# Moving the next group's first scores and their softmax inside the attention bodies of a six-stage graph network

## The chip, the cores and the metric

One core of a Trainium2 chip runs the whole program as one launch. The metric is the device time of one execution in microseconds. The engines are TensorE (PE in the rows; PEld are its weight loads), VectorE (DVE), ScalarE (ACT), GpSimd (POOL) and SyncE (SP, which issues all DMAs here). Each works through an instruction list of its own and waits on semaphores that the others raise.

## What is computed

128 graphs of 64 nodes with 384 features pass through four residual blocks. Each block normalises x, takes its positive part h, computes a graph layer on it and adds the result to x:

```
h = relu(layernorm(x));  x = x + L0(h, adj)      # two graph-convolution layers
h = relu(layernorm(x));  x = x + L1(h, adj)      # attention, 12 heads of 32, edges masked by adj
h = relu(layernorm(x));  x = x + L2(h, adj)      # two directed graph-convolution layers
h = relu(layernorm(x));  x = x + L3(h, adj)      # attention, 12 heads, adj as a bias, output projection
```

The change lies in L1 and L3. In both, q, k and v are projections of h, the scores of each graph and head are softmaxed over 64 keys and multiplied with v. L3 projects the outcome once more (Wo, bo); L1 does not.

## The kernel before, in words

**Stages and groups.** There are six stages (two gnn, att1, two gcn, att3), each a sweep over 16 groups of eight graphs. A group has T = 4 tiles of 128 rows, two graphs each. In a sweep the body for group g also prepares group F = g + 1 (its projections and first scores) and group X = g + 2 (its normalised, transposed input). A loop turn holds two bodies; 14 bodies run in the loop, and two behind it, of which the first (g = 14) still has an F. In att1 it also has an X, the first group of the stage that follows, and the last group runs in a body of its own that joins the stages (to_gcn); in att3, the last stage, the body for g = 14 has no X and that for g = 15 has neither.

**What sets the order.** The order of each engine's list is written by hand: the function a_body exists once for each engine and calls the steps in the order in which that engine runs them. An engine never goes past an instruction that waits. The waits are stated in the steps: after(engine, name, group, k) waits until step `name` of that group has been done for the k-th time.

**The steps of an attention body.** In TensorE's a_body (L890):

- part(j) (L766, through project, L664) is the j-th of ten projections of F, nine matmuls each: j = 0 to 5 give k and q, j = 6 to 9 give the values of tiles 0 to 3. They go to two PSUM banks by turns, so each waits until what stood in its bank has been read. In att3 part(7) waits for a_add_x(g,1), and part(8) in both stages for a_nat(F,1).
- a_score(g, t) (L813): 48 small matmuls, the scores of tile t, into four PSUM banks of their own. It needs q and k of the group, and that the scores of the tile before have been read.
- a_turn_p(g, t, half) (L834): three transpositions of tile t's softmax weights, which ScalarE copies out (a_keep_p, L1200).
- a_mix(g, t) (L844): the weights times the values.
- a_out(g, t, F, X) (L865): att3's output projection, nine matmuls at L885; in att1 it returns at once. Tile 1 waits for a_keep_o(g,1) and, where there is an X, for low(0).
- a_turn(F, X, c) (L756; turn_next in the body): four transpositions of X's normalised input. For c = 1 it waits in att3 for a_nat(F,0) and for c = 2 for the half of low(1) that VectorE writes.

In VectorE's a_body (L1585):

- a_nat(F, t) (nat in the body, L1491): four copies of tile t's values from PSUM with the bias added (L1502). It waits for part(6 + t).
- split_h (low in the body, L1368): the low half of X's input, one instruction at L1373 in the attention stages.
- a_soft(g, t) (L1523): three scalar_tensor_tensors (L1533) that scale the scores and add the bias, then the maximum over the keys (L1539), and in att3 a maximum of absolute values as well (L1541). GpSimd subtracts the maximum (a_shift, L526), and ScalarE takes the exponential (a_exps, L1198).
- a_sums(g, t) (L1544): in att3 the sum of the exponentials, its reciprocal and a product (L1549 to L1553), by which GpSimd then scales the weights (a_weigh, L534). In att1 it does nothing.
- a_add_x(g, t) (L1575): in att3 the output projection added to x (L1583). In att1 it does nothing.
- a_keep_o(g, t) (L1556): takes the mixed values out of PSUM; in att3 the low half for the output projection (L1561), behind ScalarE's copy (L1210).

The lists of the others in the stretch that matters: GpSimd has a_shift(g,3), a_add(g,1), a_weigh(g,3), a_shift(F,0), a_add(g,2), a_weigh(F,0); ScalarE has the copy of turn_next(1), a_keep_o(g,2), the copy of turn_next(2), a_keep_p(g,3,0), a_exps(F,0), a_keep_p(g,3,1).

The wait that binds part(7) in att3, and the one of part(8):

```
elif j == 7:
    if G.lead:
        emptied(pe, X, 0)
    else:
        after(pe, "xr", G + -1, 1)
else:
    after(pe, "evac_n", G, j - 7)
```

Here "xr" is a_add_x, "evac_n" is a_nat, and G + -1 is the group before F, so g.

Of the kernel before, what the change touches and what calls it, by code (L numbers as in the profile page):

```python
# [146 lines left out]
def graph_layers(nc, x_in, adj, adj_q, adj_t, w_all, v_all, v_cols, beta, masks, x_mid, z_mid, out):  # L147
# [5 lines left out]
    with ExitStack() as ctx:  # L153
# [487 lines left out]
        def _(pe):  # L641
# [171 lines left out]
            def a_score(g, t):  # L813
                if t == 0:
                    after(pe, "evac_t", g, 2 * C - 1)
                if t == 0 and g.lead and not g.third:
                    pe.wait_ge(st["mu"].sem, st["mu"].base[g.n])
                    pe.wait_ge(st["z1"].sem, st["z1"].base[g.n])
                elif t == 0 and g.lead:
                    pe.wait_ge(st["ex"].sem, st["ex"].base[g.n])  # L820
                    pe.wait_ge(st["dT"].sem, st["dT"].base[g.n])
                    pe.wait_ge(st["cc"].sem, st["cc"].base[g.n])
                after(pe, "stt", g, t - 1)
                for c in range(C):
                    for a in (0, 1):
                        own = slice(t * P + a * S, t * P + (a + 1) * S)
                        for j in range(HC):
                            r = slice(j * HD, (j + 1) * HD)
                            mm = nc.tensor.matmul(psum[a * S:(a + 1) * S, 2 + j, c * S:(c + 1) * S],  # L829
                                                  q_T[r, g.par, c, own], k_T[r, g.par, c, own],  # L830
                                                  start=True, stop=True, skip_group_check=True)
                done(mm, "s")

            def a_turn_p(g, t, half):  # L834
                if half == 0:
                    after(pe, "n0" if g.third else "ex", g, t)
                after(pe, "pt", g, 2 * t + half - 1)
                for i in range(3):
                    u = 2 * (3 * half + i)
                    mm = nc.tensor.transpose(tp[:, i * P:(i + 1) * P],  # L840
                                             s_sb[:, t % 2, u:u + 2].rearrange("p h k -> p (h k)"), ident)
                done(mm, "tp")
# [22 lines left out]
            def a_out(g, t, F, X):  # L865


                if not g.third:
                    return
                b = t % 2  # L870
                after(pe, "olo", g, t)
                if not F:
                    after(pe, *(("evac_n", g, T - 1), ("xr", g + -1, T - 1), ("xr", g, 0), ("xr", g, 2))[t])
                elif X:
                    after(pe, *(("evac_t", F, 2), ("lo", X, 0), ("lo", X, 2), ("xr", g, 2))[t])
                else:
                    after(pe, *(("evac_t", F, 2), ("evac_t", F, 4), ("evac_n", F, 0), ("xr", g, 2))[t])
                if t == 0:
                    pe.wait_ge(w_split, 2 * w_total(g.n))
                dst = bank_of(g + 1, Y_SLOT[t])  # L880
                s_ = w_slot(g, 3)
                k = 0
                for c in range(C):
                    for wpart, opart in ((w_hi, o_hi), (w_hi, o_lo), (w_lo, o_hi)):
                        mm = nc.tensor.matmul(dst[:, 0:H], opart[:, b, c * P:(c + 1) * P],  # L885
                                              wpart[s_][:, c, :], start=(k == 0), stop=(k == 3 * C - 1))
                        k += 1
                done(mm, "y")

            def a_body(g, F, X):  # L890
                def part(j):
                    if F:
                        a_part(F, j, X)

                def turn_next(c):
                    if X:
                        a_turn(F, X, c)

                a_turn_p(g, 0, 0)
                part(0)  # L900
                a_turn_p(g, 0, 1)
                a_score(g, 2)
                part(1)
                a_mix(g, 0)
                part(2)
                a_turn_p(g, 1, 0)
                part(3)
                a_turn_p(g, 1, 1)
                a_score(g, 3)
                a_out(g, 0, F, X)  # L910
                part(4)
                a_mix(g, 1)
                part(5)
                a_turn_p(g, 2, 0)
                turn_next(0)
                part(6)
                a_turn_p(g, 2, 1)
                a_out(g, 1, F, X)
                turn_next(1)
                if F:  # L920
                    a_score(F, 0)
                part(7)
                a_mix(g, 2)
                turn_next(2)
                a_turn_p(g, 3, 0)
                part(8)
                a_turn_p(g, 3, 1)
                if F:
                    a_score(F, 1)
                a_out(g, 2, F, X)  # L930
                if g.third:
                    a_mix(g, 3)
                    part(9)
                else:
                    part(9)
                    a_mix(g, 3)
                a_out(g, 3, F, X)
# [395 lines left out]
        def _(dve):  # L1333
# [189 lines left out]
            def a_soft(g, t):  # L1523

                b = t % 2
                third = g.third
                if t == 0 and third:
                    dve.wait_ge(ld["adj_in"].sem(g), ld["adj_in"].at(g))
                bias = adjc if third else biasc
                after(dve, "s", g, t)  # L1530
                after(dve, "tp", g, 2 * t - 3)
                for c in range(C):
                    ins = nc.vector.scalar_tensor_tensor(  # L1533
                        out=s_sb[:, b, c * HC:(c + 1) * HC], in0=s_bank[:, :, c * S:(c + 1) * S],
                        scalar=SCALE3 if third else SCALE1,
                        in1=bias[:, g.par, t].unsqueeze(1).to_broadcast([P, HC, S]), op0=ALU.mult, op1=ALU.add)
                done(ins, "stt")
                after(dve, "stt", g, t)
                done(nc.vector.tensor_reduce(mx[:, b], s_sb[:, b], AX.X, ALU.max), "mxr")  # L1539
                if third:  # L1540
                    done(nc.vector.tensor_reduce(am[:, b], s_sb[:, b], AX.X, ALU.max,  # L1541
                                                 apply_absolute_value=True), "absr")

            def a_sums(g, t):  # L1544

                b = t % 2
                if g.third:
                    after(dve, "ex", g, t)
                    done(nc.vector.tensor_reduce(sums[:, b], s_sb[:, b], AX.X, ALU.add), "sm")  # L1549
                    after(dve, "sm", g, t)  # L1550
                    done(nc.vector.reciprocal(sums[:, b], sums[:, b]), "rc")
                    after(dve, "rc", g, t)
                    done(nc.vector.scalar_tensor_tensor(out=rinv[:, b], in0=am[:, b], scalar=0.0,  # L1553
                                                        in1=sums[:, b], op0=ALU.is_gt, op1=ALU.mult), "ri")
# [30 lines left out]
            def a_body(g, F, X):  # L1585
                def low(c):
                    if X:
                        split_h(F, X, c)

                def nat(t):  # L1590
                    if F:
                        a_nat(F, t)
                if X:
                    stats_of(X, 0)
                a_sums(g, 1)
                if X:
                    stats_of(X, 1)
                a_soft(g, 2)
                if X:
                    shift_of(X)  # L1600
                a_keep_o(g, 0)
                next_w(F, X, 0)
                a_sums(g, 2)
                a_soft(g, 3)
                a_add_x(g, 0)
                if F:
                    a_bias(F)
                a_keep_o(g, 1)
                next_w(F, X, 1)
                low(0)  # L1610
                nat(0)
                a_sums(g, 3)
                a_add_x(g, 1)
                low(1)
                if F:
                    a_soft(F, 0)
                nat(1)
                a_keep_o(g, 2)
                low(2)
                if F:  # L1620
                    a_sums(F, 0)
                nat(2)
                if F:
                    a_soft(F, 1)
                a_add_x(g, 2)
                a_keep_o(g, 3)
                nat(3)
                a_add_x(g, 3)
# [273 lines left out]
```

## Time and profile before

| what | value |
|---|---|
| median of 3 runs | 3032.25 us (3029.55 to 3032.59) |
| the profiled execution | 3030.7 us, of which the span from first to last instruction is 3028.6 us |
| TensorE busy | 2803.1 us (93%) |
| VectorE busy | 1964.6 us (65%) |
| ScalarE busy | 1032.5 us (34%) |
| GpSimd busy | 950.6 us (31%) |

A row of a timeline gives the start in us, the duration in us, the engine, the source line, the operation, what it writes and reads, the shapes and how many instructions were merged; in brackets stands how long the engine had been idle before it and what ended that. Matmuls are pipelined, so a row may begin a little before the one above it has ended. "issue" is a wait that the profile does not explain. A granted clock of 1.00 is 2.4 GHz, 0.50 is 1.2 GHz.

### The profile page before, as it was taken

How to read it: one execution, taken by the hardware profiler on the slowest of the kernel's cores; microseconds unless marked ns; L12 is line 12 of the kernel's file. 1: busy time of each engine (PE TensorE's matmuls, PEld its weight loads, DVE VectorE, ACT ScalarE, POOL GpSimd, SP SyncE). 2: the span in 40 equal slices, each digit the busy share in tenths (PEclk: the TensorE clock that was granted, in tenths of full speed). 3: DMA queues.
4: the chain of work that ended last, by engine and by line, in shares of the span. 5: the costliest groups of instructions: out<-in, count | busy, mean ns of one | idle time of the engine just before them, and what ended most of it. 6: DMA issues, size and time to landing. Idle time of an engine off the chain costs nothing.

```text
span 3028.6 us, 71986 instructions
## 1 busy us (share of the span) xinstructions
PE 2803.1 (93%) x26048; PEld 2341.8 (77%) x26048; DVE 1964.6 (65%) x4550; ACT 1032.5 (34%) x1985; POOL 950.6 (31%) x874
## 2 busy tenths in 40 slices
PE   6999999999989999999999998999998899999997
PEld 5888878888877777777877777778776677777776
DVE  3444445555576666677676666677767777777775
ACT  2444433333334444443332322222222333433342
POOL 1121214444433333332010110334333343443443
PEclk9999999999999999999999999999999899999999
DMA  3222332333311211122211223222332011111111
GB/s 92 76 74 77 98 91 91 104 104 104 112 54 47 66 51 47 47 84 64 68 57 56 68 74 107 67 82 83 99 99 82 29 42 47 47 47 41 36 30 34
DMA packets 197214, 210.20 MB, mean 69 GB/s; under 512 B 72736, under 2 KB 197024, under 8 KB 197024
## 3 DMA queue, kind: packets, MB, share of 16 engines
q1 hardware_dynamic: 197024, 207.33, 22.2%
q8 instruction: 161, 2.64, 0.4%
q14 instruction: 29, 0.24, 0.0%
HBM read 131.80 MB, written 75.50 MB: 68 GB/s over the span
## 4 chain that ended last, share of the span: by engine, by line
PE 70%; DVE 15%; issue 10%; POOL 2%; ACT 2%; DVEq 1%; DMA 0%; SPq 0%; POOLq 0%; ACTq 0%
PE psum L672 26%; PE psum L675 25%; PE psum L723 3%; DVE v_x L1502 3%; PE psum L990 3%; PE psum L660 2%; PE psum L840 2%; DVE room L1650 2%; PE psum L829 2%; PE psum L885 2%; DVE room L1533 2%; DVE room L1640 2%; PE psum L739 1%; PE psum L861 1%; DVE room L1549 1%
## 5 line engine op out<-in xcount | busy, mean ns | idle before, releaser
L675 PE MATMUL psum<-fast 128*128 128x384 f32 x5760 | 1127.3, 345 | 102.1 <-DVE room L1640 46.6
L675 PEld LDWEIGHTS psum<-fast 128*128 128x128 f32 x5760 | 992.6, 189 | 196.3 <-DVE room L1640 81.5
L672 PE MATMUL psum<-fast 128*128 128x512 f32 x3456 | 871.2, 403 | 11.1 <-ACT room L1191 5.0
L672 PEld LDWEIGHTS psum<-fast 128*128 128x128 f32 x3456 | 643.5, 191 | 167.9 <-issue 22.3
L1640 DVE TENSOR_TENSOR room<-psum,rows 128x384 f32<-128x384 f32 x384 | 212.6, 554 | 232.3 <-PE psum L675 129.5
L526 POOL TENSOR_TENSOR room<-room 128x768 f32<-128x768 f32 x128 | 188.8, 1475 | 434.9 <-DVE room L1539 275.3
L589 POOL TENSOR_TENSOR room<-room,halfs 128x4 f32<-128x4 f32 x32 | 32.4, 1013 | 692.1 <-DVE room L1673 692.1
L1135 ACT ACTIVATE room<-psum 128x512 f32<-128x512 f32 x192 | 114.7, 597 | 391.5 <-PE psum L672 391.5
L660 PE MATMUL psum<-mask,z_sb 128*128 128x128 f32 x1152 | 175.4, 282 | 51.7 <-ACT z_sb L1116 22.4
L1203 ACT ACTIVATE room<-psum 128x384 f32<-128x384 f32 x256 | 124.6, 487 | 227.8 <-PE psum L840 227.7
L1502 DVE TENSOR_TENSOR v_x<-psum,rows 64x192 f32<-64x192 f32 x512 | 181.5, 355 | 28.1 <-PE psum L675 22.9
L660 PEld LDWEIGHTS psum<-mask,z_sb 128*128 128x128 f32 x1152 | 128.6, 142 | 82.3 <-issue 27.8
L1116 ACT ACTIVATE z_sb<-x_ring,negb,rstd 128x384 f32 (+1 forms) x256 | 167.9, 700 | 26.8 <-DVE negb L1365 26.8
L840 PE MATMUL psum<-mask,room 128*128 128x128 f32 x768 | 129.6, 278 | 43.9 <-issue 31.8
L1411 DVE SCALAR_TENSOR_TENSOR x_ring<-room,x_ring 128x384 f32 (+1 forms) x128 | 102.0, 796 | 101.4 <-POOL room L507 100.6
L534 POOL TENSOR_TENSOR room<-room 128x768 f32<-128x768 f32 x64 | 94.4, 1476 | 232.1 <-DVE room L1553 232.0
L1260 ACT ACTIVATE room<-psum,room 128x64 f32<-128x64 f32 x128 | 38.5, 313 | 348.3 <-DVE room L1691 348.3
L1420 DVE TENSOR_TENSOR room<-psum,rows 128x384 f32<-128x384 f32 x128 | 70.8, 554 | 128.6 <-PE psum L675 127.0
L840 PEld LDWEIGHTS psum<-mask,room 128*128 128x128 f32 x768 | 98.2, 143 | 68.8 <-issue 39.2
L507 POOL TENSOR_TENSOR room<-room,rows 128x384 f32<-128x384 f32 x128 | 143.2, 1118 | 10.0
L1380 DVE TENSOR_TENSOR fast<-room,fast 128x512 fp32r<-128x512 f32 x192 | 141.1, 735 | 6.6
L505 POOL TENSOR_TENSOR room<-room,rows 128x384 f32<-128x384 f32 x128 | 131.5, 1028 | 35.4 <-ACT room L1155 34.0
(96 smaller groups left out, 3641.4 us busy)
## 6 DMA issues: line engine op xcount, KB each, us to landing
x_ring<-x_mid SPq DMA_DIRECT2D x64, 768.0 KB, 4.5
x_mid<-x_ring SPq DMA_DIRECT2D x48, 768.0 KB, 3.9
x_ring<-x_in SPq DMA_DIRECT2D x32, 768.0 KB, 4.6
z_mid<-x_ring SPq DMA_DIRECT2D x32, 768.0 KB, 4.1
z_sb<-z_mid SPq DMA_DIRECT2D x32, 768.0 KB, 6.0
out<-x_ring SPq DMA_DIRECT2D x16, 768.0 KB, 3.9
w_raw<-w_all SPq DMA_DIRECT2D x19, 576.0 KB, 7.2
adjc<-adj SPq DMA_DIRECT2D x64, 128.0 KB, 3.8
```

Of the source, the lines that this page charges most:

```text
L505: done(nc.gpsimd.tensor_tensor(y_t[:, t], y_t[:, t], rows(g)[:, r], ALU.mult), "m1")
L507: done(nc.gpsimd.tensor_tensor(y_t[:, t], y_t[:, t], rows(g)[:, r + 1], ALU.add), "m2")
L526: done(nc.gpsimd.tensor_tensor(s_sb[:, b], s_sb[:, b], mx[:, b].unsqueeze(2).to_broadcast([P, HEADS, S]), ALU.subtract), "sub")
L660: mm = nc.tensor.transpose(by_half[:, t // 2, t % 2] if X.kind == "gnn" else dst[:, t * P:(t + 1) * P], z_sb[:, t, c * P:(c + 1) * P], ident)
L672: mm = nc.tensor.matmul(dst, wpart[s_][:, c, c_out * P:(c_out + 1) * P], hpart[:, c, 0:GT], start=(k == 0), stop=(k == 3 * C - 1))
L675: mm = nc.tensor.matmul(dst[:, 0:H], hpart[:, c, row:row + P], wpart[s_][:, c, :], start=(k == 0), stop=(k == 3 * C - 1))
L840: mm = nc.tensor.transpose(tp[:, i * P:(i + 1) * P], s_sb[:, t % 2, u:u + 2].rearrange("p h k -> p (h k)"), ident)
L1116: done(nc.scalar.activation(z_sb[:, t], x_ring[:, bass.ds(g.slot, 1), t].rearrange("p a f -> p (a f)"), ACT.Identity, bias=negb[:, t:t + 1 ...
L1203: done(nc.scalar.activation(p_T[:, 3 * half:3 * half + 3].rearrange("p i q -> p (i q)"), tp, ACT.Identity), "pt")
L1380: done(nc.vector.tensor_tensor(lo, src, hi.bitcast(F32), ALU.subtract), "lo")
L1502: ins = nc.vector.tensor_tensor(v_x[e * S:(e + 1) * S, t, a, :, e * HD:(e + 1) * HD], src[own, f].rearrange("p (i d) -> p i d", d=HD), row ...
L1640: done(nc.vector.tensor_tensor(lin3[m][:, t], bank_of(G, G_SLOT[i])[:, 0:H], rows(G)[:, m], ALU.add), "evac_n")
```

## The change

On TensorE, a_score(F, 0) comes ahead of a_out(g, 1) and turn_next(1) instead of behind them. On VectorE, a_soft(F, 0) comes directly behind nat(0), ahead of a_sums(g, 3), a_add_x(g, 1) and low(1), instead of behind these. No instruction is added or taken away, and no wait is edited.

```diff
@@ tensor, a_body
                 part(6)
                 a_turn_p(g, 2, 1)
+                if F:
+                    a_score(F, 0)
                 a_out(g, 1, F, X)
                 turn_next(1)
-                if F:
-                    a_score(F, 0)
                 part(7)
                 a_mix(g, 2)
@@ vector, a_body
                 low(0)
                 nat(0)
+                if F:
+                    a_soft(F, 0)
                 a_sums(g, 3)
                 a_add_x(g, 1)
                 low(1)
-                if F:
-                    a_soft(F, 0)
                 nat(1)
                 a_keep_o(g, 2)
```

## Rows read from the trace of the kernel before

**Rows 1.** The page: shares of the chain that ended last, by engine.
```profile
PE 70%; DVE 15%; issue 10%; POOL 2%; ACT 2%; DVEq 1%; DMA 0%; SPq 0%; POOLq 0%; ACTq 0%
```

**Rows 2.** TensorE's waits in att3, 2400 to 2980: total us, times, longest us.
```profile
PE psum L675 <- DVE v_x L1502: 16.9, 14, 1.2
PE psum L840 <- issue: 12.9, 6, 2.5
...
PE psum L675 <- DVE x_ring L1583: 8.6, 14, 0.6
```

**Rows 3.** Timeline of TensorE in one att1 body: part(7), turn_next(2), part(8).
```profile
1108.65 1.83 PE L675 MATMUL psum<-fast 128*128 128x384 f32 x9
...
1111.27 0.66 PE L660 MATMUL psum<-mask,z_sb 128*128 128x128 f32 x4
...
1112.72 1.85 PE L675 MATMUL psum<-fast 128*128 128x384 f32 x9 [0.47 <-DVE v_x L1502]
```

**Rows 4.** Timeline of VectorE in the same body: nat(0), low(1), nat(1).
```profile
1107.12 1.47 DVE L1502 TENSOR_TENSOR v_x<-psum,rows 64x192 f32<-64x192 f32 x4 [0.33 <-PE psum L675]
1108.62 0.69 DVE L1373 SCALAR_TENSOR_TENSOR fast<-psum,fast 128x512 fp32r<-128x512 f32 x1
...
1111.21 1.45 DVE L1502 TENSOR_TENSOR v_x<-psum,rows 64x192 f32<-64x192 f32 x4
```

**Rows 5.** TensorE, one att3 body: a_turn_p(g,2,1), a_score(F,0), part(7), part(8), a_out(g,3).
```profile
2650.78 0.49 PE L840 MATMUL psum<-mask,room 128*128 128x128 f32 x3
...
2653.22 0.78 PE L829 MATMUL psum<-room 32*64 32x64 f32 x48
2654.61 1.86 PE L675 MATMUL psum<-fast 128*128 128x384 f32 x9 [0.61 <-DVE x_ring L1583]
...
2659.42 1.83 PE L675 MATMUL psum<-fast 128*128 128x384 f32 x9 [1.18 <-DVE v_x L1502]
...
2667.36 1.85 PE L885 MATMUL psum<-fast 128*128 128x384 f32 x9 [0.70 <-DVE fast L1561]
```

**Rows 6.** VectorE, same body: nat(0), a_sums(g,3), a_add_x(g,1), a_soft(F,0), nat(1), a_sums(F,0).
```profile
2650.98 1.46 DVE L1502 TENSOR_TENSOR v_x<-psum,rows 64x192 f32<-64x192 f32 x4 [0.33 <-PE psum L675]
2652.47 0.95 DVE L1549 TENSOR_REDUCE room<-room 128x12 f32<-128x768 f32 x1
...
2654.00 0.56 DVE L1583 TENSOR_TENSOR x_ring<-psum,x_ring 128x384 f32 x1
...
2655.07 1.07 DVE L1533 SCALAR_TENSOR_TENSOR room<-psum,adjc 128x256 f32<-128x256 f32 x3
...
2657.91 1.45 DVE L1502 TENSOR_TENSOR v_x<-psum,rows 64x192 f32<-64x192 f32 x4
...
2660.47 0.95 DVE L1549 TENSOR_REDUCE room<-room 128x12 f32<-128x768 f32 x1
```

**Rows 7.** ScalarE, same body: a_keep_p(g,3,0) and a_exps(F,0).
```profile
2658.44 0.48 ACT L1203 ACTIVATE room<-psum 128x384 f32<-128x384 f32 x1
2659.58 0.85 ACT L1198 ACTIVATE room<-room 128x768 f32<-128x768 f32 x1 [0.66 <-POOL room L526]
```

**Rows 8.** GpSimd, same body: a_shift(F,0).
```profile
2658.07 1.47 POOL L526 TENSOR_TENSOR room<-room 128x768 f32<-128x768 f32 x1 [2.63 <-DVE room L1541]
```

**Rows 9.** TensorE behind long stops: two of att1's six loop turns, then att3's entry.
```profile
949.12 0.90 PE L840 MATMUL psum<-mask,room 128*128 128x128 f32 x3 [3.18 <-issue]
...
1288.92 0.54 PE L840 MATMUL psum<-mask,room 128*128 128x128 f32 x3 [3.02 <-issue]
...
2366.05 3.25 PE L675 MATMUL psum<-fast 128*128 128x384 f32 x9 [2.71 <-DVE v_x L1502]
```

**Rows 10.** Windows of TensorE: stretch, length, busy (count), granted clock, DMA share, GB/s.
```profile
949.10:952.20 3.10, 3.08 (x9) 0.50 0.85 266
...
2366.10:2369.30 3.20, 3.20 (x17) 0.50 0.03 5
2628.90:2632.30 3.40, 3.36 (x58) 1.00 0.88 267
```

## The prediction

> **What bounds the kernel now.** I first read the page's chain that ended last, split by engine: TensorE carries 70% of it and VectorE 15% [rows 1]. So only what moves TensorE's stream counts, and the places to look for are those where it stands still for VectorE. The change touches two stages, att1 and att3, each with 15 bodies in which a next group F exists (in att3 14 of them also with X). The view of waits for TensorE in att3 names such places: 14 waits of up to 1.2 us for a copy of values (L1502), 14 of up to 0.6 us for the residual add at L1583, and six "issue" stops of up to 2.5 us where the loop turns round [rows 2]. Then I read one body of each stage in order of time, engine by engine. The longest of each 14 waits is also their mean (8.6 / 14 = 0.6), so one body stands for all.
>
> **What moves.** In each body a_score(F,0) (48 small matmuls) goes ahead of a_out(g,1) and a_turn c=1 on TensorE; a_soft(F,0) (three scalar_tensor_tensors and one reduction, two in att3) goes to just behind a_nat(F,0) on VectorE. No work is added, no DMA is among the moved instructions, and nothing changes in the order of SyncE, GpSimd or ScalarE. What can change is who waits: VectorE takes its instructions in written order, so what a_soft is moved past comes later by its length.
>
> **att1: nothing.** There a_out, a_sums and a_add_x are empty, so on TensorE the scores change places with one transposition and on VectorE a_soft changes places with low(1) alone. a_nat(F,0) runs from 1107.12 to 1108.59, and part(7) starts 0.06 us later, at 1108.65, as now [rows 3, 4]. The scores are ready before that copy ends, since they are now one transposition earlier than scores that end before 1108.65. low(1) and a_soft together fill 1108.62 to 1111.21, when a_nat(F,1) starts [rows 4]; in either order they fill the same 2.59 us, so part(8), which waits for that copy with 0.47 us of idle time, stays at 1112.72 [rows 3]. What is late is low(1): it ends at about 1111.29 instead of 1109.31, and turn_next(2), which needs it, slips from 1111.27 to some 1111.35. Those 0.08 us fall into the 0.47 us. Sum for att1: 0; bounds ±0.1 us a body, the size of these slips, so ±1.5 us.
>
> **att3: the order on VectorE.** Here a_soft(F,0) moves past three things: a_sums(g,3), a_add_x(g,1) and low(1). It takes 2655.07 to 2657.91, that is 2.84 us [rows 6]. The new scores are no obstacle: turn_p(g,2,1) ends at 2650.78 + 0.49 = 2651.27, scores last 0.78, so they end by 2652.05, before a_nat(F,0) ends at 2650.98 + 1.46 = 2652.44 [rows 5, 6]. So a_soft starts at once, and a_sums(g,3) and a_add_x(g,1) come 2.84 us later: a_add_x at 2656.84 instead of 2654.00 [rows 6].
>
> TensorE's part(7) writes the PSUM bank that a_add_x(g,1) reads, and already waits 0.61 us for it [rows 5]. It therefore moves from 2654.61 to 2657.45. Before it TensorE has the same work as now, which ends near 2654.61 - 0.61 = 2654.0 in either order; its idle time there grows from 0.61 to between 3.2 and 3.45 us. Nothing covers it: all behind part(7) is queued behind it.
>
> **What of the 2.84 us comes back.** Two later waits can absorb some: 1.18 us before part(8) and 0.70 us before a_out(g,3) [rows 5]. But they don't simply subtract, because VectorE's later work now waits for TensorE in turn:
> - a_nat(F,1) reads part(7)'s result. It starts at 2657.91 now; with part(7) ending at 2657.45 + 1.86 it starts at 2659.3, and part(8) at about 2660.85, 1.43 us later than 2659.42. 1.41 us are absorbed so far.
> - Behind part(7) come a_mix(g,2), turn_next(2) and a_turn_p(g,3,0), all 2.84 us later. ScalarE's copy of the last, now at 2658.44, comes at 2661.28, and its exponential of F's first tile behind it. Today that exponential had to wait another 0.66 us for GpSimd and starts at 2659.58 [rows 7], when GpSimd's subtraction (2658.07 + 1.47) is done [rows 8]. GpSimd has its a_weigh(g,3) in front of that subtraction; a_weigh needs a_sums(g,3), which is later, so the earlier softmax does not bring the subtraction forward. It is done well before the copy, though, so the exponential starts at the copy's end, 2661.28 + 0.48 = 2661.76, 2.18 us later than now.
> - a_sums(F,0) waits for it: 2662.65 instead of 2660.47 [rows 6]. From there VectorE runs without a gap to the low half that a_out(g,3) waits for, so a_out(g,3) starts at 2667.36 + 2.18 [rows 5]. TensorE works on from there to the next body without a wait on VectorE, so nothing is recovered.
>
> So each body loses 2.18 us: 2.84 less the 0.66 that the exponential no longer waits for GpSimd. The body without X has no turn_next and no low, but the same waits; I count it alike. Sum: 15 x 2.18 = 32.7 us.
>
> **The clock.** The new idle time would be the longest inside an att3 body, and the trace of before shows no such stop there, so I price what follows one by bounds. Where att1's loop turns round TensorE stands still for about 3 us, six times (the first, 3.18, and the last, 3.02, are in the rows) [rows 9]; behind the first the granted clock is 0.50, that is 1.2 GHz instead of 2.4 [rows 10]. Behind the 2.71 us stop at the entry to att3 the clock is 0.50 too, and the nine matmuls of a part take 3.25 us against 1.83 to 1.86: some 1.42 us more [rows 5, 9, 10]. Of att3's own turns, with stops of up to 2.5 us [rows 2], most keep the full clock, as at 2628.90 [rows 10]. Bounds per body: 0 (the clock holds) and 1.83 us (those 1.42, and 0.41 by which three transpositions are slower behind the first stop, 0.90 against 0.49 [rows 5, 9]). The new stop is nearest to the six, and the slowed work (part(7), a_mix, turn_next, a_turn_p) is all on the path found above. It is nearer to the upper bound, but some stops may escape, so I take 1.3 us a body: 15 x 1.3 = 19.5 us. The Trainium skill (TensorE: Matmul & The Clock Gate, HAM oscillation — how this bites in real kernels) warns of idle gaps only from about the longest length that I expect here; by that rule the clock would hold and the sum would stay at 32.7. The trace differs: the gaps of 2.71 to 3.18 us in the rows were followed by half clock.
>
> **Sum.** 32.7 + 19.5 = 52.2 us on the profiled execution's 3030.7 us: 3082.9. That execution is 1.55 us below the median of the three runs (3032.25), which is inside their spread; I say 3083.
>
> **Rivals.**
> - *The clock holds.* The stop is there but TensorE keeps 2.4 GHz: 3030.7 + 32.7 = 3063. For it: most of att3's turns keep the clock. Against it: those stops are shorter.
> - *The delay is absorbed.* The two later waits give back all they have: 2.84 - 1.18 - 0.70 = 0.96 us a body, 15 times: 14 us, 3045; with VectorE's other idle times it could end within 0.2%. Against it: the chain through ScalarE's exponential to a_sums(F,0).
> - *Faster.* Scores and softmax ahead of the waits end TensorE's two waits, 0.61 and 1.18 us in each of 14 bodies: 25 us, 3006. It would hold if part(7) were let go by something that stands before a_soft, so from the point at which a_add_x(g,1) is not the last to release its bank. The trace names a_add_x as the releaser in all 14 [rows 2], and a_soft now stands in front of it.
>
> **How the numbers follow.** Forecast 0.75, clock holds 0.13, absorbed 0.09 (a third of it within 0.2%), faster 0.03. A measurement of this kernel tells about 0.2%, 6 us, from no change. That gives slower 0.94, same 0.03, faster 0.03. The range goes from a little under the second case, 3058, to every stop at 1.83 us: 32.7 + 27.5 = 60.2, with three more slow turns of att3's loop at 1.42 64.5, so 3095.
>
> **What would show it.** In the changed kernel the wait of part(7) for L1583 should be over 3 us, 14 or 15 times, and that of part(8) for L1502 close to nothing. A pair of att3 bodies should last some 6 to 7 us longer and a pair in att1 the same as now. The granted clock behind the new stop should be 0.50 in most bodies. VectorE should show new idle time in front of a_nat(F,1), and in front of the reduction at L1549. I'm wrong if part(7)'s wait stays under 1 us (then a_add_x was not what held it), or if att1's bodies change by more than 0.1 us.

## The result, and the profile after

The changed kernel takes 3082.22 us (median of four executions) against 3031.37 us for the kernel before beside it; the ratio is 1.0167 (95% interval 1.0151 to 1.0182), so by the ratio it is slower by some 51 us (46 to 55). One of the four executions took 9697.56 us, which counts in that median but not in the ratio; the others took 3078.41, 3079.07 and 3085.36 us, the last of them the profiled one. The forecast was 3083, slower.

Where the time went is seen first in TensorE's waits. The view of waits for TensorE in att3 (2400 to 3030, since the stage now ends later) reads:

```profile
PE psum L675 <- DVE x_ring L1583: 45.5, 14, 3.3
PE psum L885 <- DVE fast L1561: 18.3, 14, 1.4
PE psum L840 <- issue: 12.9, 6, 2.3
```

The wait of part(7) for the residual add (L1583) has grown from 0.6 to 3.25 us in each of 14 bodies, and the wait of part(8) for a copy of values (L1502) is gone [rows 2]. Further on a_out(g,3) now waits longer for the low half (L1561): 1.2 to 1.4 us, where it waited 0.70 [rows 5].

One body in which the clock held answers to [rows 5 to 8]. Its timeline on TensorE (a_turn_p(g,2,1), the scores, part(7), part(8), a_out(g,3)):

```profile
2489.11 0.49 PE L840 MATMUL psum<-mask,room 128*128 128x128 f32 x3
2489.53 0.78 PE L829 MATMUL psum<-room 32*64 32x64 f32 x48
...
2495.78 1.83 PE L675 MATMUL psum<-fast 128*128 128x384 f32 x9 [3.25 <-DVE x_ring L1583]
...
2499.18 1.85 PE L675 MATMUL psum<-fast 128*128 128x384 f32 x9
...
2507.74 1.84 PE L885 MATMUL psum<-fast 128*128 128x384 f32 x9 [1.30 <-DVE fast L1561]
```

On VectorE (nat(0), the softmax's first step, the sums, the add, nat(1), the sums of F's first tile):

```profile
2489.30 1.46 DVE L1502 TENSOR_TENSOR v_x<-psum,rows 64x192 f32<-64x192 f32 x4 [0.35 <-PE psum L675]
2490.80 1.09 DVE L1533 SCALAR_TENSOR_TENSOR room<-psum,adjc 128x256 f32<-128x256 f32 x3
...
2493.65 0.94 DVE L1549 TENSOR_REDUCE room<-room 128x12 f32<-128x768 f32 x1
...
2495.17 0.56 DVE L1583 TENSOR_TENSOR x_ring<-psum,x_ring 128x384 f32 x1
...
2497.65 1.47 DVE L1502 TENSOR_TENSOR v_x<-psum,rows 64x192 f32<-64x192 f32 x4 [1.33 <-PE psum L675]
...
2500.83 0.95 DVE L1549 TENSOR_REDUCE room<-room 128x12 f32<-128x768 f32 x1 [0.42 <-ACT room L1198]
```

On ScalarE (a_keep_p(g,3,0), a_exps(F,0)) and on GpSimd (a_weigh(g,3), a_shift(F,0)):

```profile
2499.58 0.49 ACT L1203 ACTIVATE room<-psum 128x384 f32<-128x384 f32 x1
2499.95 0.85 ACT L1198 ACTIVATE room<-room 128x768 f32<-128x768 f32 x1
...
2495.14 1.48 POOL L534 TENSOR_TENSOR room<-room 128x768 f32<-128x768 f32 x1 [9.82 <-DVE room L1553]
2496.57 1.47 POOL L526 TENSOR_TENSOR room<-room 128x768 f32<-128x768 f32 x1
```

To compare with the body of before, count from the start of nat(0) in each. The add starts 5.87 us behind it (before: 3.02), nat(1) 8.35 (6.93), the sums of F's first tile 11.53 (9.49), a_out(g,3) 18.44 (16.38). So the add is 2.85 us late, and 2.06 us of that are still there at the end of the body. The softmax did start at once, 0.03 us behind nat(0), and the subtraction on GpSimd did not come earlier: it stands behind a_weigh, which waited 9.82 us for the late sums.

The clock is the second part. In windows of TensorE just behind the new stop (stretch, length, busy with the count of its instructions, granted clock, DMA share, GB/s) the body above kept 1.00, while others ran at 0.50:

```profile
2495.80:2499.10 3.30, 3.30 (x39) 1.00 0.02 5
2538.40:2541.70 3.30, 3.30 (x26) 0.50 0.00 0
2586.20:2589.50 3.30, 3.30 (x30) 0.50 0.02 5
2859.30:2862.60 3.30, 3.30 (x31) 0.50 0.02 5
```

What this costs is read from the start of part(7) to the start of part(8), between which TensorE now waits for nothing. In the body above that is 3.40 us, in the two below 5.92 and 4.86:

```profile
2720.34 3.25 PE L675 MATMUL psum<-fast 128*128 128x384 f32 x9 [3.25 <-DVE x_ring L1583]
...
2726.26 1.83 PE L675 MATMUL psum<-fast 128*128 128x384 f32 x9
...
2858.62 2.76 PE L675 MATMUL psum<-fast 128*128 128x384 f32 x9 [3.25 <-DVE x_ring L1583]
...
2863.48 1.83 PE L675 MATMUL psum<-fast 128*128 128x384 f32 x9
```

Of the 14 bodies with X, three take 3.40 to 3.42 us, nine 4.81 to 4.87 and two 5.92. Against full clock that is 18.1 us in all, 1.3 a body. The body without X loses some 2 us more.

The same view of the stretches behind the six turns of att3's loop shows half clock at five of them; in the kernel before it is two of the six (the first two rows below; the one in [rows 10], 2628.90, kept the full clock). The two rows of before, then the six of the changed kernel:

```profile
2546.40:2549.50 3.10, 3.10 (x25) 0.50 0.45 119
2877.40:2880.60 3.20, 3.20 (x41) 0.50 0.49 125
...
2467.90:2470.90 3.00, 3.00 (x61) 1.00 0.75 212
2555.50:2558.70 3.20, 3.20 (x9) 0.50 0.87 260
2647.70:2650.90 3.20, 3.20 (x10) 0.50 0.59 160
2739.90:2743.00 3.10, 3.10 (x9) 0.50 0.59 157
2828.60:2831.80 3.20, 3.20 (x10) 0.50 0.83 245
2920.80:2924.00 3.20, 3.20 (x10) 0.50 0.58 154
```

A turn at half clock takes 1.6 us longer: from the end of the stop to the next a_mix it is 7.4 us instead of 5.85.

The two stages can be told apart by the first and the last scores (L829). In att3 they lie 698.8 us apart, before 643.3 (the row of before first):

```profile
L829 PE MATMUL psum<-room x3036: 211/217/365, 2360.7 to 3004.0; 32*64 32x64 f32 x190
L829 PE MATMUL psum<-room x3072: 211/217/362, 2361.3 to 3060.1; 32*64 32x64 f32 x192
```

In att1 they lie 528.9 us apart (872.3 to 1401.2; before 527.1, 873.0 to 1400.1). The span of the profiled execution has grown by 54.7 us; att3 is 55.5 us longer, att1 1.8, and the rest of the program 2.6 shorter.

### The profile page after: what moved, and what is told of

Read it like the earlier page. It is cut to its first block, busy times and chain, and to the rows that moved or that the text cites. A ratio compares the mean times of both kernels' runs of the same rounds, so it can differ in the third digit from the quotient of the medians.

```text
span 3083.3 us, 71986 instructions
## 1 busy us (share of the span) xinstructions
PE 2831.3 (92%) x26048; PEld 2364.1 (77%) x26048; DVE 1970.5 (64%) x4550; ACT 1030.1 (33%) x1985; POOL 948.7 (31%) x874
## 4 chain that ended last, share of the span: by engine, by line
PE 71%; DVE 14%; issue 9%; ACT 2%; POOL 2%; DVEq 1%; DMA 0%; SPq 0%; POOLq 0%; ACTq 0%
PE psum L672 26%; PE psum L675 26%; PE psum L723 3%; PE psum L660 3%; PE psum L990 3%; DVE v_x L1502 2%; PE psum L840 2%; DVE room L1650 2%; PE psum L885 2%; PE psum L829 2%; DVE room L1533 2%; DVE room L1640 2%; PE psum L852 1%; PE psum L739 1%; PE psum L861 1%
## 5 line engine op out<-in xcount | busy, mean ns | idle before, releaser
L1502 DVE TENSOR_TENSOR v_x<-psum,rows 64x192 f32<-64x192 f32 x512 | 181.7, 355 | 59.2 <-PE psum L675 53.9
L1203 ACT ACTIVATE room<-psum 128x384 f32<-128x384 f32 x256 | 124.6, 487 | 229.9 <-PE psum L840 229.9
L840 PE MATMUL psum<-mask,room 128*128 128x128 f32 x768 | 131.8, 282 | 43.1 <-issue 31.4
L840 PEld LDWEIGHTS psum<-mask,room 128*128 128x128 f32 x768 | 100.6, 146 | 68.1 <-issue 40.2
L1380 DVE TENSOR_TENSOR fast<-room,fast 128x512 fp32r<-128x512 f32 x192 | 142.2, 741 | 6.6
L507 POOL TENSOR_TENSOR room<-room,rows 128x384 f32<-128x384 f32 x128 | 143.1, 1118 | 10.1
L1347 DVE BATCH_NORM_STATS2 stats<-x_ring 128x6 f32 (+1 forms) x256 | 128.5, 549 | 21.2 <-DMA beta_sb<-beta 13.8
```

Source lines behind the costliest of these rows:

```text
L507: done(nc.gpsimd.tensor_tensor(y_t[:, t], y_t[:, t], rows(g)[:, r + 1], ALU.add), "m2")
L840: mm = nc.tensor.transpose(tp[:, i * P:(i + 1) * P], s_sb[:, t % 2, u:u + 2].rearrange("p h k -> p (h k)"), ident)
L1203: done(nc.scalar.activation(p_T[:, 3 * half:3 * half + 3].rearrange("p i q -> p (i q)"), tp, ACT.Identity), "pt")
L1347: done(nc.vector.bn_stats(stats[:, t], x_ring[:, bass.ds(g.slot, 1), t].rearrange("p a f -> p (a f)")), "bn")
L1380: done(nc.vector.tensor_tensor(lo, src, hi.bitcast(F32), ALU.subtract), "lo")
L1502: ins = nc.vector.tensor_tensor(v_x[e * S:(e + 1) * S, t, a, :, e * HD:(e + 1) * HD], src[own, f].rearrange("p (i d) -> p i d", d=HD), row ...
```

## The experiments

The theory was that in att3 the softmax, now in front of the residual add on VectorE, holds part(7); that 2.1 us of it stay in each body (31 us); and that the stop lowers the clock (20 us). The rivals were that TensorE's new order, the late low(1) or the late sums cost the time, and that the slow clock falls into time that is waited anyway.

**1. The scores alone.** TensorE's half of the change on the kernel before.

```diff
                 a_turn_p(g, 2, 1)
+                if F:
+                    a_score(F, 0)
                 a_out(g, 1, F, X)
                 turn_next(1)
-                if F:
-                    a_score(F, 0)
```

> Only TensorE's move, VectorE's list as before. Theory (the loss comes from the softmax standing in front of the residual add on VectorE): the scores are early and nobody uses it; part(7) in att3 waits 0.6 us as before; 3031 us, within 4 us. Rival (TensorE's new order costs, by itself or by delaying the output projection and the transposition): some or all of the 51 us, so 3045 to 3082.

Measured: 3044.05 us against 3029.48, ratio 1.0056 (1.0039 to 1.0073). The theory missed: this half has a price of its own. The rows are of an execution of 3037.05 us, the shortest of four that go up to 3052.69. The reason is seen on VectorE in att1, where low(1) now has idle time in front of it:

```profile
1103.36 1.46 DVE L1502 TENSOR_TENSOR v_x<-psum,rows 64x192 f32<-64x192 f32 x4 [0.33 <-PE psum L675]
1105.61 0.69 DVE L1373 SCALAR_TENSOR_TENSOR fast<-psum,fast 128x512 fp32r<-128x512 f32 x1 [0.79 <-ACT fast L1124]
```

The transposition comes behind the scores, so ScalarE's copy of it comes later, and low(1), which still stands ahead of the softmax, waits 0.79 us for it with everything behind. TensorE's wait before part(8) grows to 1.23 us in att1 and to 1.6 in att3. In the change itself the softmax fills that gap: the wait of part(8) is gone in att3 and 0.39 us in att1. So this price is not part of the 51 us.

**2. The softmax alone.** VectorE's half of the change on the kernel before.

```diff
                 nat(0)
+                if F:
+                    a_soft(F, 0)
                 a_sums(g, 3)
                 a_add_x(g, 1)
                 low(1)
-                if F:
-                    a_soft(F, 0)
                 nat(1)
```

> Only VectorE's move, TensorE's list as before, so the softmax behind the first copy waits for scores that end about 1.6 us after that copy. Theory: in att3 the add and part(7) come some 4.4 us later than before instead of 2.84, a body loses 3.6 us and the clock falls behind the longer stop: 15 x 3.6 + 21 = 75 us over before, 3105, 3090 to 3115; att1 unchanged. Rival (the two moves cost separately, so that this one costs the 51 us less the 14 of the scores alone): 3060 to 3070.

Measured: 3123.90 us against 3029.59, ratio 1.0312 (1.0295 to 1.0329). The direction and the wait are the theory's, and the stop of part(7) is as long as its place in the list says:

```profile
PE psum L675 <- DVE x_ring L1583: 61.2, 12, 5.1
```

The size was 19 us short, and the time lies outside the range: behind a stop of 5.1 us more time ran at half clock than I had allowed for (all 15 stops are followed by a slowed part(7), all six turns are slow; mean granted clock in att3 0.93, against 0.95 in the change and 0.99 before, over 2400 to 2980). The two halves do not add up to the whole: 15 and 94 us alone, 51 together.

**3. The softmax behind the add.** Both moves, but on VectorE a_soft(F, 0) goes past low(1) only.

```diff
                 nat(0)
-                if F:
-                    a_soft(F, 0)
                 a_sums(g, 3)
                 a_add_x(g, 1)
+                if F:
+                    a_soft(F, 0)
                 low(1)
```

> Both moves, but on VectorE the softmax goes behind the sums of (g,3) and the residual add of (g,1), so that it passes low(1) alone. Theory: part(7) is released as before, low(1) ends some 0.7 us later than turn_next(2) would like and that is absorbed before part(8): 3031 us, within 5 us. Rival (the loss comes from low(1), through the late transposition): stays near 3082.

Measured: 3030.69 us against 3029.48, ratio 1.0002 (0.9993 to 1.0012): the whole loss is gone. low(1) is late, as expected, and TensorE waits 0.73 us for it ahead of turn_next(2), but gets that back at part(8):

```profile
2657.45 1.86 PE L675 MATMUL psum<-fast 128*128 128x384 f32 x9 [0.41 <-DVE x_ring L1583]
...
2660.89 0.66 PE L660 MATMUL psum<-mask,z_sb 128*128 128x128 f32 x4 [0.73 <-DVE fast L1373]
...
2662.26 1.86 PE L675 MATMUL psum<-fast 128*128 128x384 f32 x9 [0.39 <-DVE v_x L1502]
```

In att1 this kernel is the changed one, instruction for instruction, so it also shows that the change costs at most some 4 us there (the interval ends at 1.0012).

**4. The sums ahead, the add behind.**

```diff
                 nat(0)
+                a_sums(g, 3)
                 if F:
                     a_soft(F, 0)
-                a_sums(g, 3)
                 a_add_x(g, 1)
```

> Both moves, but on VectorE the sums of (g,3) stand ahead of the softmax, the residual add of (g,1) behind it. Theory (the add holds part(7), the sums have slack): part(7) still waits about 3.3 us, a body of att3 still loses some 2.1 us and the clock falls as often: 3082 us, 3074 to 3088. Rival (the sums, through GpSimd's scaling of the weights, carry the loss): 3031 to 3045.

Measured: 3077.02 us against 3029.48, ratio 1.0153 (1.0136 to 1.0170), with part(7) waiting 3.2 us, as the theory had it:

```profile
PE psum L675 <- DVE x_ring L1583: 41.7, 13, 3.2
```

With the sums in time nearly all of the loss is still there. Runs 3 and 4 differ only in the place of the add, so passing the add is what costs.

**5. The add ahead, sums and low(1) behind.**

```diff
                 nat(0)
+                a_add_x(g, 1)
                 if F:
                     a_soft(F, 0)
                 a_sums(g, 3)
-                a_add_x(g, 1)
                 low(1)
```

> Both moves, but on VectorE the residual add of (g,1) goes ahead of the softmax; the sums of (g,3) and low(1) stay behind it. Theory: part(7) is let go at once (wait under 0.4 us), but low(1) holds turn_next(2) for about 2 us and the sums hold GpSimd, so the sums of (F,0) come 1.9 us later: 29 us, and no stop of 3 us, so the clock holds: 3058, 3050 to 3066. Rival (all of the loss hangs on part(7)'s wait): 3030 to 3035.

Measured: 3067.32 us against 3029.59, ratio 1.0123 (1.0106 to 1.0140), 1 us above the range. part(7) goes at once, and the next in the line takes over, with a stop of the length that was worked out:

```profile
PE psum L660 <- DVE fast L1373: 27.2, 13, 2.1
...
PE psum L675 <- DVE x_ring L1583: 5.5, 14, 0.4
```

The theory's other half failed: it had the clock hold, but behind this stop of 2.1 us the next projection is slowed in 7 of 14 bodies, and five of the six turns of the loop are slow. One of the seven:

```profile
2631.62 0.66 PE L660 MATMUL psum<-mask,z_sb 128*128 128x128 f32 x4 [2.07 <-DVE fast L1373]
...
2632.99 2.98 PE L675 MATMUL psum<-fast 128*128 128x384 f32 x9
```

So taking one wait away was not enough. In run 3 passing low(1) alone was free, so here it is the sums, or the sums and low(1) together; no run has the sums alone behind. Of the places tried only the one behind both sums and add is free.

**6. The stop filled.** The changed kernel, with matmuls that nobody reads in the new stop, first 20, then 12, in att3 only. Nothing of the computation is left out.

```diff
                 turn_next(1)
+                if F and g.third:
+                    for _ in range(12):
+                        nc.tensor.matmul(psum[:, 7, H:H + P], ident, ident, start=True, stop=True,
+                                         skip_group_check=True)
                 part(7)
```

> The changed kernel with 20 idle-filling 128x128 matmuls in att3 between turn_next(1) and part(7), written to columns of a PSUM bank that nobody reads; they last some 2.7 us, less than the 3.25 us for which part(7) waits. Theory (31 us of the loss are waiting, 20 us the clock behind the stop): the clock holds inside the bodies, part(7) starts at the same place, 3063 us, 3057 to 3069. Rival (the slow clock falls into time that is waited anyway, and the whole loss is waiting): 3078 to 3085. Should the filling itself delay part(7), 20 times its excess shows in part(7)'s start.

> The filled kernel with 12 filling matmuls instead of 20. In the run with 20 each ran as two passes, so the filling took 4.63 us and moved part(7) by some 0.9 us; 12 take about 2.8 us, less than the wait of 3.25 us. Theory (waiting 31 us, clock about 20 us): part(7) waits about 0.4 us for the add, no slow clock inside the bodies, 3060 us against 3029.5 of before, 3054 to 3066. Rival (waiting alone makes the loss, the slow clock is hidden): 3075 to 3082.

Measured: with 20, 3072.11 us against 3029.48, ratio 1.0140 (1.0123 to 1.0157), outside the range because the filling took 4.63 us, longer than the stop, and part(7) starts 7.20 us behind its scores instead of 6.25; with 12, 3065.00 against 3029.59, ratio 1.0114 (1.0097 to 1.0131). The rows (L1587 and L1565 are L1583 and L1561, four lines further down) show the filling and a_out(g,3) of the run with 20, then the filling, part(7) and a_out(g,3) of the run with 12:

```profile
2493.80 4.63 PE L924 MATMUL psum<-mask 128*128 128x128 f32 x40
...
2510.14 1.83 PE L885 MATMUL psum<-fast 128*128 128x384 f32 x9 [1.29 <-DVE fast L1565]
```

```profile
2495.95 2.84 PE L924 MATMUL psum<-mask 128*128 128x128 f32 x24
2499.39 1.86 PE L675 MATMUL psum<-fast 128*128 128x384 f32 x9 [0.59 <-DVE x_ring L1587]
...
2511.36 1.85 PE L885 MATMUL psum<-fast 128*128 128x384 f32 x9 [1.30 <-DVE fast L1565]
```

With 12, part(7) is released by the same add, and starts 6.26 us behind its scores, 6.25 us in the changed kernel, so nothing has moved. But the clock behind it is 1.00 (window 2499.40 to 2502.80), and from part(7) to part(8) each of the 14 bodies takes 3.39 to 3.42 us. By the ratios some 16 us of the 51 are gone with that alone, and their intervals do not overlap, so the slow clock inside the bodies was a cost by itself.

How large it is the rows tell better, because this run pays more at the turns of att3's loop: all six are slow instead of five, and TensorE stands still there for 17.1 us instead of 12.9. Its att3 is 683.1 us from the first to the last scores, 15.7 less than in the changed kernel, although the turns cost 4.2 + 1.6 us more. So the filling has saved some 21 us, about the 20 that the rows of the changed kernel give for the bodies. What is left is the waiting, 15 x 2.06 = 31, and the turns. Why their stops are longer here is open.

**7. Other orders.** A new order in att1 alone, then in both stages. In att1, VectorE copies the second values ahead of the softmax, and ScalarE's exponentials go behind the copies that TensorE waits for:

```diff
                 low(0)
                 nat(0)
+                if not g.third:
+                    low(1)
+                    nat(1)
+                    if F:
+                        a_soft(F, 0)
+                    low(2)
+                    a_keep_o(g, 2)
+                    nat(2)
+                    nat(3)
+                    if F:
+                        a_soft(F, 1)
+                    a_keep_o(g, 3)
+                    return
...
-                a_exps(g, 1)
                 turned(0)
                 a_keep_p(g, 0, 1)
+                a_exps(g, 1)
...
-                if F:
-                    a_exps(F, 0)
                 a_keep_p(g, 3, 1)
                 a_keep_o(g, 3)
+                if F:
+                    a_exps(F, 0)
```

(In the run for att1 alone the two moves on ScalarE are made in att1 only.)

> The kernel before with the new order in att1 alone: on VectorE the second copy of values goes ahead of the softmax of (F,0), the third and fourth ahead of that of (F,1), and on ScalarE the exponentials behind the copies that TensorE waits for; att3 as before. Theory (the 0.47 us before part(8) in att1 hangs on the softmax in front of that copy): the wait goes, 8 to 10 us less, 3020, 3015 to 3024. Rival (the later softmax is waited for at the next body's start): 3027 to 3035.

Measured: 3020.24 us against 3030.25, ratio 0.9969 (0.9958 to 0.9979). All 14 waits of part(8) in att1 are gone; the loop's turns are all that TensorE waits for there.

For att3 the order on VectorE became nat(0), add of (g,1), sums of (g,3), low(1), nat(1), low half of (g,2), low(2), softmax of (F,0), nat(2), add of (g,2), low half of (g,3), sums of (F,0), nat(3), softmax of (F,1), add of (g,3); with the order for att1 this is values_first.

> Another order on the kernel before (TensorE's list unchanged): on VectorE the residual add goes ahead of the sums, the second copy of values ahead of the softmax of (F,0), and in att3 the softmaxes behind what TensorE waits for; on ScalarE the exponentials stand behind the copies that TensorE waits for. Theory (TensorE's waits for VectorE, 2.5 us in an att3 body and 0.5 in an att1 body, can be ordered away, less some 0.7 us of new waits for the scaled weights at the start of every other att3 body): 30 us less, 3000, 2990 to 3012. Rival (what is put behind becomes the next wait: the exponentials and sums of F's first tiles at the next body's start): 3022 to 3040.

Measured: 3059.84 us against 3029.59, ratio 1.0102 (1.0085 to 1.0119), a miss and slower, above the rival's range too. The view of waits for TensorE in att3 and the add of (g,3) on VectorE name the new wait:

```profile
PE psum L672 <- DVE x_ring L1583: 25.0, 13, 2.4
```

```profile
2591.56 0.56 DVE L1583 TENSOR_TENSOR x_ring<-psum,x_ring 128x384 f32 x1 [2.65 <-POOL x_ring L546]
```

GpSimd's bias add stood behind the subtraction of F's second tile, which now came later. values_adds puts the bias adds of tiles 2 and 3 ahead:

```diff
                 a_add(g, 1)
+                if g.third:
+                    a_add(g, 2)
+                    a_add(g, 3)
                 a_weigh(g, 3)
...
-                a_add(g, 2)
+                if not g.third:
+                    a_add(g, 2)
...
-                a_add(g, 3)
+                if not g.third:
+                    a_add(g, 3)
```

> The run values_first with one more edit: in att3 GpSimd adds the output bias to x for tiles 2 and 3 before it scales the weights of (g,3), instead of behind the subtraction of F's tiles. Theory (values_first lost in att3 because the last residual add waited 2.65 us for GpSimd's bias add of tile 3, which stood behind the subtraction of (F,1), and part(1) of the next body waited for that add): the 2.4 us wait of part(1) goes, the waits for the scaled weights shrink, TensorE's 2.5 us a body are gained less about 0.5: 2995, 2985 to 3012. Rival (the softmax of F's tiles is now too late for the next body whatever GpSimd does): 3025 to 3050.

Measured: 3023.82 us against 3030.25, ratio 0.9984 (0.9975 to 0.9993), a miss between the two ranges. The named wait went, but ScalarE's normalisation, waiting 4.29 us for VectorE, became the next one (L1208 is L1203 and L845 is L840, five lines further down):

```profile
PE psum L845 <- ACT room L1208: 19.6, 13, 1.9
PE psum L845 <- POOL room L534: 16.2, 13, 2.0
```

values_norms moves that normalisation behind the copy, in att3 only:

```diff
                 a_keep_o(g, 0)
-                norms(0)
+                if not g.third:
+                    norms(0)
                 turned(2)
                 a_keep_p(g, 1, 0)
+                if g.third:
+                    norms(0)
                 a_exps(g, 2)
```

> The run values_adds with one more edit: in att3 ScalarE's first normalisation of X goes behind its copy of the weights of (g,1). In values_adds that normalisation waits on ScalarE for VectorE's shift, 4.29 us in the body read, and the copy behind it made TensorE wait up to 1.9 us, 13 times. Theory: that wait goes, 19.6 us less than values_adds, 3004, 2997 to 3012. Rival (the normalisation itself, or the exponentials behind it, become the next wait of the same size): 3018 to 3026.

Measured: 3016.27 us against 3028.03, ratio 0.9957 (0.9944 to 0.9971), the fastest of all, 12 us below the kernel before, but not the 3004 expected. Of 19.6 us of waits only 5 to 8 were gained (by the difference to the kernel before, or directly); most of the rest went into a wait for the last residual add, which the next projection needs:

```profile
PE psum L845 <- POOL room L534: 17.7, 14, 2.0
PE psum L677 <- DVE x_ring L1591: 12.8, 13, 1.2
```

Most of the gain over the kernel before is att1's: att1_values alone is at 0.9969, and the intervals overlap, so a gain in att3 is not shown.

## Why the prediction was right

- *What bounds the kernel.* TensorE's stream, stopped by VectorE at a few places. Runs 1 to 5 change nothing but the order, and in each the wait that comes or goes on TensorE has the sign of the change in time.
- *att1: nothing.* Right for the bodies in the loop: a pair of them lasts 67.5 to 68.2 us between two turns, before 67.6 to 68.3, and the wait before part(8) went from 0.47 to 0.39 us, which is the 0.08 by which turn_next(2) was to slip. Not so behind the loop: in the body for g = 14, whose X belongs to the next stage, an instruction of low(1) (L1380) lasted 1.84 us instead of 0.69, and part(8) waits 2.10 us instead of 1.03. About the 1.8 us of att1 lie there, a little over the bound of 1.5; run 3 has the same wait (2.07) and measures 1.0002.
- *att3, the order on VectorE.* The add was to come 2.84 us later and came 2.85 later; the stop was to be between 3.2 and 3.45 us and is 3.25, 14 times. Run 3 against run 4 shows that passing the add is what costs.
- *What comes back.* nat(1) was to be 1.4 us late and is 1.42; its wait for part(7) is there (1.33), part(8)'s wait is gone. Of the 2.84 us 2.18 were to stay and 2.06 stayed. Most of the 0.12 is ScalarE's: the exponential starts 0.37 us behind the start of the copy, before that copy's 0.49 us are over, and I had it start at the copy's end. So this term was 15 x 2.06 = 31 instead of 32.7.
- *The clock.* 19.5 us were counted, 1.3 in each of 15 bodies, and nothing for the loop's turns. In the profiled execution the bodies cost 18.1 + 2 = 20 us, so the term was right in size. Its make-up was not: three of 14 stops cost nothing, nine about 1.45, and two cost 2.52, more than the upper bound of 1.83, which left out that a_mix and turn_next are slowed as well (0.92 to 1.55 and 0.66 to 1.12 us). That the mean is 1.3 is in part luck. Three more of the loop's turns are slow, at 1.6 us each 5 us, which the sum had left out and only the range's upper end held. Waiting, bodies and turns (31 + 20 + 5) make up the 55.5 us that att3 lost there; forecast were 32.7, 19.5 and 0. That 3083 lies so close to the measured time is luck too: a term left out against one too large, and executions that differ by 7 us among themselves. Why more of the turns fall is open. The longer wait of a_out(g,3) ahead of them does not do it by itself: in the run filled with 20 it is 1.29 us as well, and one turn of the six is slow. The rival that the clock holds is refused by its 0.50 in the rows and by the filled runs. The Trainium skill (TensorE: Matmul & The Clock Gate, HAM oscillation — how this bites in real kernels) warns of idle gaps a little longer than these; here gaps of 3.25 us were followed by slowed matmuls in 11 of 14 bodies, and the measurement decides.
- *The rivals.* That the delay is absorbed fails at the chain named against it, through the exponential to the sums of (F,0): VectorE idles 0.42 us there for ScalarE. The faster case fails at its own point: the add does release part(7).

Several expectations on the way were wrong. The scores alone cost 15 us, because I followed what the scores do and not what a transposition behind them holds up (low(1) on VectorE). The softmax alone cost 19 us more than expected, and run 5 lost its clock behind stops of 2.1 us, where I had expected it to hold. And each of the new orders for att3 put a wait that I had not counted in the place of the one removed, on GpSimd, then on ScalarE, then in front of the next projection.

## What to carry to other kernels

On engines that take their lists in order, moving a step earlier delays everything it passes by its whole length: look among the passed steps for the one that another engine is already waiting for, since there the delay becomes idle time of that engine (0.61 to 3.25 us here). Then follow the delay through the other engines until it meets slack; here two waits on the way (1.18 and 0.70 us) looked as if they could absorb most of it, but the step behind them was itself fed by the delayed engine. The move that paid here, att1_values, goes the other way: it puts the softmax behind what the bounding engine needs next, the second copy of values.

## What the runs showed of the hardware

- A stop has a price beyond its length: filling 2.84 of the 3.25 us with matmuls that nobody reads gave back some 16 us of the 51 (ratio 1.0167 to 1.0114), 21 by the rows of att3, though part(7) started no earlier.
- The filling was 20 matmuls of 128 x 128 in fp32 in the program; the trace has 40, at 4.63 us, 0.116 us each, while each of the transpositions of the same tile shape stands in it once.
- Stops of 2.1 us can be followed by half clock too: in run 5 seven of 14 such stops were, with nine matmuls taking 2.82 to 3.25 us instead of 1.83 to 1.86 (granted clock 0.51 from 2455.80 to 2459.00). Neither there nor behind the stops of 3.25 us does a run show why some are and others are not.
